# Score maxima as two bf16 parts in one 32-row block, subtracted by a bf16 pick matrix, in a cross-attention kernel on one core

## The reference, cut to what matters

```python
scores = jnp.einsum('bqhd,bkhd->bhqk', q, k) * scale
probs = jax.nn.softmax(scores, axis=-1)          # once over text keys, once over image keys
out = jnp.einsum('bhqk,bkhd->bqhd', probs, v)    # img_x + txt_x
```

## Time and profile before

| | us |
|---|---|
| median of 3 runs (1544.85 to 1547.99) | 1547.46 |
| span of the profiled execution (the only time given for it) | 1546.9 |
| TensorE busy | 1515.9 (98%) |
| VectorE busy | 1186.4 (77%) |
| ScalarE busy | 712.3 (46%) |
| GpSimd busy | 665.3 (43%) |
| share of the chain that ended last: TensorE, ScalarE, VectorE | 88%, 4%, 3% |

### The profile page before, as it was taken

One profiled execution on the slowest core, in us unless ns is written; L12 is line 12 of the kernel. 1 busy time (PEld: TensorE's weight loads), 2 busy tenths in 40 slices (PEclk: granted clock), 3 DMA queues, 4 the chain that ended last, 5 costly groups with the idle time before them and its releaser, 6 DMA issues.

```text
span 1546.9 us, 41175 instructions
## 1 busy us (share of the span) xinstructions
PE 1515.9 (98%) x16220; PEld 1179.0 (76%) x16220; DVE 1186.4 (77%) x1884; ACT 712.3 (46%) x1458; POOL 665.3 (43%) x727
## 2 busy tenths in 40 slices
PE   8999999999999999999999999999998999999997
PEld 6777777777777777777777777777776787778897
DVE  6765888888887888888788888788887587554986
ACT  5874444444444344444444444434446124556431
POOL 3443434444434444433444443444445592114752
PEclk9999999999999999999999999999999999999999
DMA  8963111221111221111122111122114524010000
GB/s 265 337 201 124 52 52 53 78 61 50 56 50 50 69 69 54 55 50 50 57 74 61 50 56 50 50 69 72 51 37 128 193 109 164 28 55 29 1 1 24
DMA packets 70199, 121.04 MB, mean 78 GB/s; under 512 B 21840, under 2 KB 36528, under 8 KB 68608
## 3 DMA queue, kind: packets, MB, share of 16 engines
q1 hardware_dynamic: 69312, 117.54, 23.4%
q0 software_dynamic: 832, 2.75, 0.6%
HBM read 89.93 MB, written 30.34 MB: 78 GB/s over the span
## 4 chain that ended last, share of the span: by engine, by line
PE 88%; ACT 4%; DVE 3%; DMA 2%; issue 1%; SPq 1%; POOL 1%; ACTq 0%; POOLq 0%; DVEq 0%
PE ps L1488 21%; PE ps L1490 18%; PE ps L1489 18%; PE ps L1638 8%; PE ps L1603 6%; PE ps L1549 3%; PE ps L1578 3%; PE ps L1609 2%; PE ps L1837 2%; PE ps L1854 2%; ACT prob L809 2%; DMA q_dram<-q_turned 2%; PE ps L1846 1%; ACT prob L807 1%; PE ps L1613 1%
## 5 line engine op out<-in xcount | busy, mean ns | idle before, releaser
L555 POOL TENSOR_TENSOR prob_img<-prob 128x448 f32<-128x448 f32 x124 | 145.3, 1172 | 211.6 <-ACT prob L809 211.6
L522 POOL TENSOR_TENSOR ctx_lo<-ctx_raw,ctx_hi 128x472 fp32r<-128x472 f32 (+1 forms) x62 | 111.6, 1825 | 243.5 <-ACT ctx_hi L750 243.5
L1122 DVE RECIPROCAL rec<-ps 128x224 f32<-128x224 f32 x128 | 199.2, 1556 | 7.5 <-PE ps L1638 3.8
L807 ACT ACTIVATE prob<-ps 119x448 f32<-119x448 f32 x128 | 69.6, 544 | 196.3 <-PE ps L1603 196.3
L1111 DVE TENSOR_REDUCE top<-ps 112x4 f32<-112x1028 f32 x128 | 156.3, 1221 | 0.0
L1116 DVE SCALAR_TENSOR_TENSOR prob_img<-prob,ones_last,prob_img 23x448 f32<-23x448 f32 x124 | 84.8, 684 | 72.9 <-POOL prob_img L555 70.9
L783 ACT ACTIVATE sq_junk<-proj 128x513 bf16<-128x513 f32 (+1 forms) x96 | 61.2, 637 | 169.1 <-DVE proj L1090 169.1
L1110 DVE TENSOR_REDUCE top<-ps 112x4 f32<-112x472 f32 x128 | 83.1, 649 | 61.3 <-PE ps L1578 61.2
L1603 PE MATMUL ps<-q_all,k_all 32*128 32x112 f32 (+1 forms) x3072 | 125.2, 274 | 1.9 <-issue 1.9
L809 ACT ACTIVATE prob<-ps 128x896 f32<-128x896 f32 x128 | 117.0, 914 | 0.0
L1488 PE MATMUL ps<-w_v_img_hi,ctx_hi 128*128 128x512 f32 x256 | 110.9, 433 | 0.0
(11 more groups left out here) (339 smaller groups left out, 4334.1 us busy)
## 6 DMA issues: line engine op xcount, KB each, us to landing
ctx_raw<-in_ctx_dram SPq DMA_DIRECT2D x32, 748.0 KB, 4.2
xh_dram<-xh SPq DMA_DIRECT2D x32, 448.0 KB, 3.1
xc<-in_xT_dram SPq DMA_DIRECT2D x28, 256.0 KB, 4.5
q_dram<-q_turned SPq DMA_DIRECT2D x28, 256.0 KB, 4.6
q_all<-q_dram SPq DMA_DIRECT2D x32, 224.0 KB, 3.1
out_dram<-out_sb SPq DMA_DIRECT2D x32, 224.0 KB, 2.3
xh<-in_x_dram SPq DMA_DIRECT2D x31, 224.0 KB, 2.9
proj<-in_x_dram SPq DMA_DIRECT2D x21, 256.0 KB, 5.2
```

What stands on the lines that cost most here:

```text
L522: nc.gpsimd.tensor_tensor(ctx_lo[:, :, cols], ctx_raw[:, :, cols], ctx_hi[:, :, cols].bitcast(F32), ALU.subtract).then_inc(ctx_lo_done, 1)
L555: nc.gpsimd.tensor_tensor(prob_img[:, g % 2], prob[:, g % 2, 1, :], prob[:, g % 2, 2, :], ALU.add).then_inc(img_summed, 1)
L807: nc.scalar.activation(prob[0:CHUNK_C, g % 2, 0, :].rearrange("p (j q) -> p j q", j=GH), ps[0:CHUNK_C, 2:6, 0:L], ACT.Exp).then_inc(exp_do ...
L1122: nc.vector.reciprocal(rec[:], bank[:, 2:4]).then_inc(norm_step, 1)
```

## The change

`topT`, `pick_c` and `pick_img` become bf16. So that little is lost by it, a new step on VectorE, `split_top(i, e)`, splits each maximum into two parts. It copies the four fresh columns of each head (112 partitions, 16 elements) to a bf16 tile `top_hi`, waits for that, and writes the difference to columns 8 and up of the same 32-column block of `top[e]`. The transpose carries both parts, ScalarE's copy rounds both to bf16, and the pick table now has a -1 in row r and in row 8+r, so that the same matmul subtracts both parts. The count and the shapes of the TensorE instructions stay. `turn_top(i, e)` on TensorE now waits for the split instead of for the maxima. The two `gap` tiles only keep the addresses of the other tiles.

```diff
-        pick_c = p1("pick_c", [P, NG, CHUNK_C], F32R)
-        pick_img = p1("pick_img", [P, NG, P], F32R)
+        pick_c = p1("pick_c", [P, NG, CHUNK_C], BF16)
+        pick_img = p1("pick_img", [P, NG, P], BF16)
+        p1("pick_gap", [P, NG * (CHUNK_C + P) // 2])
-        topT = [p1(f"topT{e}", [P, L], F32R) for e in range(2)]
+        topT = [p1(f"topT{e}", [P, L], BF16) for e in range(2)]
+        top_hi = p1("top_hi", [L, GH, 4], BF16)
+        p1("top_gap", [P, L - 8])
+            def split_top(i, e):
+                rows = top[e][:].rearrange("l (j r) -> l j r", j=GH)
+                high, low = rows[:, :, 4 * e:4 * e + 4], rows[:, :, 2 * NG + 4 * e:2 * NG + 4 * e + 4]
+                dve.wait_ge(s_done, 4 * i + 2 * e + 2)
+                nc.vector.tensor_copy(top_hi[:], high).then_inc(top_rounded, 1)
+                dve.wait_ge(top_rounded, 2 * i + e + 1)
+                nc.vector.tensor_tensor(low, high, top_hi[:], ALU.subtract).then_inc(top_split, 1)
                 group_max(i, 1)
+                split_top(i, 0)
                 group_max(i, 3)
+                split_top(i, 1)
             def turn_top(i, e):
-                pe.wait_ge(s_done, 4 * i + 2 * e + 2)
+                pe.wait_ge(top_split, 2 * i + e + 1)
-    arrays["pick_rows"] = -(np.arange(P)[:, None] % HD == np.arange(2 * NG)[None, :]).astype(f)
+    parts = (np.arange(2 * NG)[None, :], 2 * NG + np.arange(2 * NG)[None, :])
+    arrays["pick_rows"] = -sum((np.arange(P)[:, None] % HD == part).astype(f) for part in parts)
```

More of the change, by code:

```diff
@@ L307, in build @@
         rope_loaded = sem("rope_loaded")
+        top_rounded, top_split = sem("top_rounded"), sem("top_split")
         ring_loaded = [sem(f"ring_loaded{j}") for j in range(3)]
```

## The result

The changed kernel takes 1595.8 us (median of 4 runs, 1593.2 to 1598.5) where the one before takes 1547.7 beside it: a ratio of 1.031 [1.030, 1.033]. The prediction said 1539.4 and gave slower a chance of 0.08.

The account below looks back on a forecast made before the run. TensorE, holding 88% of the chain, was taken as the bound, its scores_T blocks by weight loading. 1546.9 - 9.0 + 0.9 = 1538.8 us span, plus 0.6 for the median: 1539.4 us; forecast's own range 1536.9 to 1542.0, overall 1533.0 to 1546.6.

Parts of the forecast that it names:

- TensorE's part: In the scores_T blocks, shorter bf16 weight loads gain 0.07 us a block, 128 x 0.07 = 9.0 us.
- the step through the block: Load starts in one scores_T block: after the change 0, 0.055, 0.16, 0.26 (pick_img), 0.355; fourth set previously 0.42.
- the type change at no cost: On TensorE, switching between fp32 and bf16 matmuls was taken not to empty the array and costed at nothing.
- VectorE's part: Two instructions added to each of 64 splits, 0.66 to 0.75 us a split; covered except in the last batch, 0.9 us.
- Two instructions are added to each of 64 splits: On VectorE, a split is 0.16 + 0.16 + 0.16 + 0.18 = 0.66 us with waits, priced from L1102 and L1144.
- hidden: Each batch's first split, before add_residual, where VectorE idles 1.16 us for TensorE, was to cost nothing.
- GpSimd's slack is short by some 0.2 at worst ... Nothing reaches TensorE: After the second split, GpSimd's delay makes VectorE's sum wait, but add_tail(0) ends early enough for TensorE's matmul.
- the 0.75 that I allowed: In VectorE's queue behind the second split, add_bias(n, 1), score and the rest all come 0.75 us late.
- The last batch: Without cover, its second transpose waits 0.66 us more and its first some 0.25; together 0.9 us, once.
- A change of type empties the array: Rival on TensorE: three type changes a block cost 0.2 us each, 77 us in all, giving 1616; chance 0.02.
- The split comes late: Rival: second split exceeds 0.97 us, turn_top(1) stalls TensorE in 31 batches, up to 25.7 us, 1565; chance 0.06.
- What would show it: Signs: pick_c load about 127 ns, pick_img 141, block 0.99 us; wrong if L1585 waits for VectorE 31 times.

Follow-up runs that it names:

- e1: Changed kernel with bf16 types only: no split, maxima one rounded 16-bit part; 1541.2 us, ratio 0.9952 to the kernel before.
- e3: Changed kernel, but GpSimd's longer ctx_lo subtraction (image columns) waits for the batch's first split; 1553.2 us, ratio 1.0029 to the kernel before.
- e4: Changed kernel, but VectorE copies the high maxima to PSUM and subtracts from that copy; 1562.6 us, ratio 1.0096 to the kernel before.
- e7: Changed kernel with the first split's subtraction done twice, first into an unread scratch tile; 1597.8 us, ratio 1.0322 to the kernel before.
- e8: Changed kernel with the high part kept as an fp32 tile, the low part then zero; 1591.7 us in one run.
- e5: Changed kernel without each batch's first split (those maxima one rounded part), second split kept; 1547.4 us, ratio 0.9999 to the kernel before.
- e9: Changed kernel with GpSimd's image subtraction after the first split and the loop's second split behind add_bias(n, 1); 1543.0 us, ratio 0.9969 to the kernel before.
- e6: Changed kernel without each batch's second split (those maxima one rounded part), first split kept; 1586.1 us, ratio 1.0246 to the kernel before.
- e10: e9 without the last batch's two splits (its maxima one rounded part); 1541.0 us, ratio 0.9954 to the kernel before.

## Why the prediction was wrong

**TensorE's part was right.** Per block 0.065 to 0.07 us was worked out and 0.065 measured; e1, which is that part alone, took 1541.2 us inside my own range of 1536.9 to 1542.0. So were the step through the block and the type change at no cost. Of the two terms, `pick_c`'s load fell from 173 to 125 ns (127 expected) and `pick_img`'s from 187 to 101 (141 expected); by the prediction's stepping the second makes no difference, because its matmul waits for the third set's stream in either case. The next load behind it does start at 0.356, where that stepping put it. The Trainium skill, "TensorE: Matmul & The Clock Gate", section "Weight-path perf modes — Fast Weight Load (FWL) and DoubleRow", gives the faster load to 128 columns alone. The 128-column load did shrink most; but the 119-column one shrank too, so that fewer columns gain nothing, as the prediction read the rule, doesn't fit here.

**The step that failed** is in VectorE's part: "Two instructions are added to each of 64 splits", priced at 0.16 and 0.18 us each from L1102 and L1144, with nothing asked about what GpSimd does at that moment. The first split of a batch was then called hidden, because `add_residual` behind it has 1.16 us of idle time. Its two instructions take 0.23 + 2.30 us, and what is late is not `add_residual` but `turn_top(0)`, which I never looked at for the first split: TensorE waits 1.2 to 1.4 us there in each batch. The cover at `turn_top(0)` was not what was short: in e3, where the split takes 0.23 + 0.17 us, TensorE doesn't wait there in mid-loop. What failed is the price. It also accounts for VectorE's busy time, which grew by 89 us and not by the forecast 22: 31 times the 2.1 us too much are 66 of the difference. The cause is shown by four runs: the same instruction takes 0.17 when GpSimd starts later (e3), 0.17 when one input is in PSUM (e4), 0.16 right behind the stalled one (e7), and 2.30 with other types (e8). The Trainium skill states it, in "SBUF — State Buffer", section "Who interferes with whom": VectorE's second pair of SBUF ports is shared with GpSimd, and one instruction keeps it until it has ended. By that section an instruction with two SBUF inputs stands behind GpSimd's whole instruction if GpSimd reads SBUF, and one with a single SBUF input doesn't, outside the modes that use both pairs of ports; 2.30 against 0.17 us agree. I had not weighed it, though GpSimd's instruction stands in the trace of before, over the place where the first split would come (VectorE's maxima of group 1 are done at 701.71 there):

```profile
700.71 3.60 POOL L522 TENSOR_TENSOR ctx_lo<-ctx_raw,ctx_hi 128x472 fp32r<-128x472 f32 x2 [7.82 <-ACT ctx_hi L750]
```

The opening says that the engines meet only at semaphores. For VectorE and GpSimd that is wrong: here they meet at SBUF too.

The rows of before held a warning: `scale_k` on text keys (118 x 512) takes 1704 ns in mean and on image keys (128 x 512) 748, in the same line. A twofold difference between near-equal forms is something to be explained before an instruction is priced from a neighbour. The same trace holds the explanation: `scale_k` on text keys in the first two batches and in the 30 others (minimum, median, maximum in ns), and what GpSimd runs beside the one at 710.53, which takes 1.77 us:

```profile
L1096 DVE SCALAR_TENSOR_TENSOR proj<-proj,rstd,w_txt x2: 742/748/753, 114.2 to 141.2; 118x512 f32<-118x512 f32 x2
L1096 DVE SCALAR_TENSOR_TENSOR proj<-proj,rstd,w_txt x30: 1752/1769/1773, 174.6 to 1145.9; 118x512 f32<-118x512 f32 x30
710.46 1.29 POOL L559 TENSOR_TENSOR out_sb<-xh 112x512 f32<-112x512 f32 x1
```

The first two batches have no `output` on GpSimd, and no GpSimd instruction overlaps `scale_k` there: 0.75 us. In all 30 others `out_sb` began 0.1 us before it.

**The sentence that failed in second place** is "GpSimd's slack is short by some 0.2 at worst ... Nothing reaches TensorE". The delay of `add_bias(n, 1)` was about 0.45, under the 0.75 that I allowed. But it puts `scale_k` onto GpSimd's image sum, which gets longer, from 1.16 to 1.53, and not just later. `add_tail` is then late, and TensorE waits for it: 0.32 us a batch when alone (e5), 10 us over the loop. That the overlap is what stretches the sum rests on e9, where both are gone together, and on other sums in the traces, whose length goes with the overlap. In the kernel before, a sum takes 1.13 to 1.16 us beside the reciprocal, which reads PSUM, and 1.23 to 1.31 where `add_tail` (inputs in SBUF) covers its first 0.2 to 0.3. In the changed kernel it takes 1.53 where `scale_k` covers 0.5, and 1.63 where `add_tail` covers 0.6:

```profile
748.14 0.68 DVE L1128 SCALAR_TENSOR_TENSOR prob_img<-prob,ones_last,prob_img 23x448 f32<-23x448 f32 x1
748.20 1.63 POOL L559 TENSOR_TENSOR prob_img<-prob 128x448 f32<-128x448 f32 x1 [1.36 <-ACT prob L813]
```

No run moves the overlap alone.

**The last batch** was to cost 0.9 us. It cost 3.5 + 1.7 ahead of its second transpose, and the part behind gave 5.0 back. That the net, 0.2, is not far from 0.9 is luck.

**The rivals.** In number "A change of type empties the array", with 1616, lies nearest to 1595.8, by luck: in e1 the types alone are a gain. In mechanism "The split comes late" came nearest, with 1565 at its worst and the price at the second split. Its mechanism, a transpose waiting for a split, is the one seen, but at the first split and four times as long as the rows priced it. My argument against it, that no small instruction in the rows takes over 0.18, asked for the wrong property: size instead of who else is at SBUF. "What would show it" named the right sign, a transpose that waits 31 times.

**Added up**, a batch: 33.49 - 0.26 for the blocks, + 1.50 for the first split (e6), + 0.20 for the second on top = 34.93.

## What to carry to other kernels

Before a VectorE instruction with two SBUF inputs, or an SBUF copy, is placed on a chain that another engine waits for, look at what GpSimd runs at that time: a 16-element operation here took as long as GpSimd's instruction still had to run (2.3 us), a copy even as long as the rest of two (3.7), and it shows as the instruction's own duration, not as idle time. Remedies seen here are to start the GpSimd instruction behind it (e3), to read one input from PSUM (e4), or not to need the operation. e1, at the price of coarser maxima of one rounded part, and e10, with two parts in all batches but the last, are faster than both kernels, at 0.995; e9 keeps both parts everywhere at 0.997. These are gains of half a per cent and less. A delay worked out on one engine should be laid over the neighbours' timeline once more, since it may make two instructions meet that did not meet before.

## What had not been expected of the hardware

A subtraction of 112 x 16 elements took 2.30 us beside a GpSimd instruction of 2.4 us and 0.175 alone; a copy with rounding of the same size, from SBUF to SBUF, took 3.72 us beside two GpSimd instructions of 4.68 together, where a copy to PSUM at the same point of e4 took 0.18. The other direction shows as well, if less surely: GpSimd's sum of 128 x 448 took 1.53 us beside VectorE's `scale_k` and 1.16 without. A bf16 weight load of 32 x 128 took 101 ns where the 32 x 119 one took 125; the one with more columns was the shorter. The two stand at different places of the block, the 119-column one first, so this doesn't show that the columns are the reason.
